# A convolution step rewritten on rows that ScalarE normalises, its mean put back at the end, in a four-pass transformer layer on one core

## The reference

```
x = x + attention(layernorm(x))                # with a second layer norm, gamma and beta inside
x = x + ffn(layernorm(x))                      # -> x2
x = x + s4d(layernorm(x))                      # -> x3: convolution along the axis of length 2
x = x + ffn(layernorm(x))                      # -> x4, the output

ffn(h)  = ((silu(h @ Wg * sg)) * (h @ Wu * su)) @ Wd * sd     # weights rounded to fp8 values
s4d(z)[0] = z[0] * (k0 + D)
s4d(z)[1] = z[1] * (k0 + D) + z[0] * k1        # only two taps, since the axis has two entries
```

## Time and profile before

| | us |
|---|---|
| median of three runs | 134.78 |
| the three runs | 134.71, 134.78, 136.53 |
| profiled execution, its own time | 134.78 |
| its span, first to last instruction | 133.0 |

### The profile page before, as it was taken

One profiled execution on the slowest core, in us unless ns is written; L12 is line 12 of the kernel. 1 busy time (PEld: TensorE's weight loads), 2 busy tenths in 40 slices (PEclk: granted clock), 3 DMA queues, 4 the chain that ended last, 5 costly groups with the idle time before them and its releaser, 6 DMA issues.

```text
span 133.0 us, 2063 instructions
## 1 busy us (share of the span) xinstructions
PE 117.5 (88%) x666; PEld 77.2 (58%) x666; DVE 104.6 (79%) x234; ACT 71.6 (54%) x132; POOL 88.6 (67%) x162
## 2 busy tenths in 40 slices
PE   5997979959999999999999997959999929999940
PEld 5884648528668768665577453446454517455630
DVE  0499999999973776857958999999999998456362
ACT  3225376817965468859653564954554633573500
POOL 2255899999998888963241756989999660049521
PEclk9999999999999999999999999999999999999999
DMA  4999800000000000000000000000000000002204
GB/s 99 312 327 384 267 4 2 0 0 5 0 2 0 2 0 5 0 0 0 0 0 5 0 0 0 0 2 5 0 0 0 0 2 0 5 0 79 79 0 158
DMA packets 5666, 5.80 MB, mean 44 GB/s; under 512 B 1124, under 2 KB 5144, under 8 KB 5656
## 3 DMA queue, kind: packets, MB, share of 16 engines
q1 hardware_dynamic: 4776, 5.65, 12.6%
q10 hardware_dynamic: 816, 0.02, 0.3%
q0 software_dynamic: 64, 0.02, 0.1%
HBM read 4.63 MB, written 1.05 MB: 43 GB/s over the span
## 4 chain that ended last, share of the span: by engine, by line
PE 43%; DVE 42%; issue 5%; ACT 3%; POOL 3%; DMA 2%; DVEq 0%; POOLq 0%; ACTq 0%
PE psum L1153 16%; PE psum L1168 8%; PE psum L1092 7%; DVE stats L652 6%; PE psum L1067 5%; DVE fused L917 4%; DVE scaled_down L865 3%; DVE down_raw L741 3%; DVE grid L732 3%; PE psum L1032 3%; DVE normed L888 3%; DMA x_in<-in_x 2%; DVE h_rows L906 2%; DVE grid L733 2%; PE psum L1114 2%
## 5 line engine op out<-in xcount | busy, mean ns | idle before, releaser
L436 POOL TENSOR_TENSOR f_tail<-fused,f_head 128x512 f16<-128x512 f32 x12 | 14.2, 1181 | 18.0 <-ACT f_head L614 18.0
L603 ACT ACTIVATE gated<-psum,scales 128x512 f32<-128x512 f32 x24 | 16.4, 683 | 15.8 <-PE psum L1153 15.8
L1168 PE MATMUL psum<-down,f_head 128*128 128x256 bf16 x96 | 22.0, 273 | 0.1
L1168 PE MATMUL psum<-down,f_tail 128*128 128x256 bf16 x96 | 22.0, 273 | 0.0
L917 DVE SCALAR_TENSOR_TENSOR fused<-psum,up_scales_fit,gated 128x512 f32<-128x512 f32 x24 | 17.6, 740 | 4.5 <-PE psum L1153 3.4
L614 ACT ACTIVATE f_head<-fused 128x512 f16<-128x512 f32 x24 | 15.0, 625 | 9.8 <-DVE fused L917 9.6
L1153 PE MATMUL psum<-h_head,up 128*128 128x512 f16 x48 | 14.3, 379 | 0.8 <-DVE fused L917 0.7
L924 DVE TENSOR_TENSOR f_tail<-fused,f_head 128x512 f16<-128x512 f32 x12 | 9.5, 790 | 6.2 <-ACT f_head L614 6.2
L1153 PE MATMUL psum<-h_tail,gate 128*128 128x512 f16 x48 | 14.3, 379 | 0.0
L1153 PE MATMUL psum<-h_tail,up 128*128 128x512 f16 x48 | 14.3, 379 | 0.0
L1153 PE MATMUL psum<-h_head,gate 128*128 128x512 f16 x48 | 14.3, 379 | 0.0
(11 more groups left out here) (169 smaller groups left out, 265.8 us busy)
## 6 DMA issues: line engine op xcount, KB each, us to landing
x_in<-in_x SPq DMA_DIRECT2D x4, 256.0 KB, 4.5
out<-x_in SPq DMA_DIRECT2D x4, 256.0 KB, 2.1
qkv_sb<-in_qkv SPq DMA_DIRECT2D x3, 256.0 KB, 4.3
gate_raw<-in_gate_w SPq DMA_DIRECT2D x1, 768.0 KB, 6.0
up_raw<-in_up_w SPq DMA_DIRECT2D x1, 768.0 KB, 7.8
down_raw<-in_down_w SPq DMA_DIRECT2D x1, 768.0 KB, 9.5
wo_sb<-in_o_proj SPq DMA_DIRECT2D x1, 256.0 KB, 5.3
down_scale_all<-in_down_scale SPq DMA_DIRECT2D x1, 128.0 KB, 9.3
```

What stands on the lines that cost most here:

```text
L436: pool.tensor_tensor(f_tail[:, m, :], fused[:, m % FUSED, :], f_head[:, m, :], ALU.subtract).then_inc(f_tail_by_pool, 1)
L603: act.activation(gated[:, m % 2, :], psum[:, BANK_GATE[m % 2], :], ACT.Silu, scale=gate_scales[:, m:m + 1]).then_inc(gated_ready, 1)
L1168: last = pe.matmul(column(BANK_DOWN[t // 2], H * (t % 2), H), part[:, m, t * P:t * P + P], down16[:, m, :], start=(m == 0 and t % 2 == 0 a ...
```

## The change

- x3 is kept without x2's mean. With z = (x2 - mean) * rstd and std = 1/rstd, x2 + tap0 * z = mean + (tap0 + std) * z. The layer norm behind it doesn't see the mean. So VectorE has one step per tile, (tap0 + std) * z, in place of two.
- z comes from ScalarE for all eight tiles (`z_rows`), in place of four (`x_lag`), and earlier in the pass. GpSimd computes std in `inverse_std` (one instruction more), and the negative mean term every time.
- The second tap's product now reads z of batch 0, and VectorE adds it in pass 2 (four additions more), in place of GpSimd's four `add_lag`.
- GpSimd adds all four residuals of pass 1 and 2; VectorE's `add_x1` goes. ScalarE normalises all four tiles for the next pass; VectorE's `norm_rows` go.
- The mean is put back in pass 3: ScalarE adds it for six tiles (`put_mean_back`), and VectorE's last two additions (`add_x3`) take it as a third operand. GpSimd's four residuals of pass 3 wait for ScalarE's first four.
- Voiding moves from VectorE's list in pass 2 to its list in pass 3, behind the first `fuse` and ahead of the four `scaled_down`; TensorE's sum for it moves from behind m = 1 of pass 2 to behind m = 0 of pass 3.
- In passes 1 and 2 GpSimd's tails are m = 1, 2, 4 in place of 1, 3, 4.

```
-                    residual(0, x2, x1, (first, first + 2, first + 3), x2_by_pool)
-                    inverse_std(2, first, 2, negative_mean=(n == 1))
+                    residual(0, x2, x1, range(first, first + T), x2_ready)
+                    inverse_std(2, first, 2, negative_mean=True, with_std=True)
+                    inverse_std(2, first + 2, 2, negative_mean=True, with_std=True)
+                    tail(n, POOL_TAILS[n][0])
+                    inverse_std(3, first, 2, negative_mean=True)
+                    tail(n, POOL_TAILS[n][1])
+                    inverse_std(3, first + 2, 2, negative_mean=True)
+                    tail(n, POOL_TAILS[n][2])
                     if n == 1:
...
+                        for t in range(T):
+                            lag_tap(t)
                 else:
-                    tail(n, POOL_TAILS[0])
+                    tail(n, POOL_TAILS[n][0])
                     if n == 3:
+                        pool.wait_ge(mean_back, T)
                         residual(1, x4, x3, range(T), x4_by_pool)
...
+            def z_rows(k):
+
+                act.wait_ge(shift_ready[2], k + 1)
+                act.activation(normed[:, k, :], x2[:, k, :], ACT.Identity, scale=rstd[:, 2, k:k + 1],
+                               bias=neg_mean_rstd[:, 2, k:k + 1]).then_inc(z2_ready, 1)
+
+            def put_mean_back(k):
+
+                act.activation(x3[:, k, :], x3[:, k, :], ACT.Identity, scale=1.0,
+                               bias=mean_var[:, 2, k, 0:1]).then_inc(mean_back, 1)
...
+                if n == 3:
+                    put_mean_back(T)
+                    put_mean_back(T + 2)
+                head(n, 5)
...
+            def convolve(tiles):
 
                 dve.wait_ge(taps_loaded, 1)
                 for k in tiles:
...
+                    dve.wait_ge(std_ready, k + 1)
+                    dve.wait_ge(z2_ready, k + 1)
+                    ins = dve.scalar_tensor_tensor(out=x3[:, k, :], in0=taps_all[:, 0, :], scalar=std[:, k:k + 1],
+                                                   in1=normed[:, k, :], op0=ALU.add, op1=ALU.mult)
...
                 for k in tiles:
...
+                    dve.wait_ge(lag_ready, k - T + 1)
+                    dve.tensor_tensor(x3[:, k, :], x3[:, k, :], x_lag[:, k - T, :], ALU.add).then_inc(x3_ready, 1)
...
             for n in range(2 * B):
                 if n >= 1:
                     h_tails(n)
+                if n == 3:
+
+                    fuse(n, 0)
+                    void_beyond()
+                if n >= 1:
...
-                    if n == 2 and m == 1:
+                    if n == 3 and m == 0:
                         pe.wait_ge(beyond_ready, 1)
...
-                if n == 2:
-                    pe.wait_ge(beyond_read, 1)
```

More of the change, by code:

```diff
@@ L119, in hybrid_layer @@
         one_rstd = sb("one_rstd", [P, K])
+        std = sb("std", [P, K])
         mean_rstd = sb("mean_rstd", [P, 4, K])
@@ L270, in load_s4d, with inverse_std @@
                                array.rearrange("(c p) n -> p c n", p=P)).then_inc(loaded, 16)
-            def inverse_std(n, k, count=1, twice=False, negative_mean=False):
+            def inverse_std(n, k, count=1, twice=False, negative_mean=False, with_std=False):
                 pool.wait_ge(stats_ready[n], k + count)
@@ L442, in residual, with lag_tap @@
                     pool.tensor_tensor(new[:, k, :], scaled_down[:, k, :], old[:, k, :], ALU.add).then_inc(ready, 1)
-            def lag_tap():
+            def lag_tap(t):
                 pool.wait_ge(taps_loaded, 1)
[L447 to L453, removed]
+                pool.wait_ge(z2_ready, t + 1)
+                pool.tensor_tensor(x_lag[:, t, :], normed[:, t, :], taps_all[:, 1, :], ALU.mult).then_inc(lag_ready, 1)
             for n in range(2 * B):
@@ L609, in _ @@
                 gate(n, 0)
[L610 to L631, removed]
@@ new lines, in _ @@
+                gate(n, 1)
+                head(n, 0)
+                if n == 0:
+                    copy_taps()
+                gate(n, 2)
+                head(n, 1)
+                if n == 0:
+                    for k in (T, T + 1):
+                        normalise(1, k, x1)
+                if n in (1, 2):
+                    z_rows(tiles[0])
+                    z_rows(tiles[1])
+                if n == 3:
+                    for k in range(T):
+                        put_mean_back(k)
@@ new lines, in _ @@
+                gate(n, 3)
+                if n in (1, 2):
+                    z_rows(tiles[2])
+                    z_rows(tiles[3])
+                head(n, 2)
+                if n == 0:
+                    for k in (T + 2, T + 3):
+                        normalise(1, k, x1)
+                gate(n, 4)
+                head(n, 3)
+                if n in (1, 2):
+                    normalise(3, tiles[0], x3)
+                    normalise(3, tiles[1], x3)
+                gate(n, 5)
+                head(n, 4)
```

134 lines of the change are left out of this document (58 added, 76 removed).

## The result

The changed kernel takes 130.81 us in the median (130.73 to 131.11, four runs); run beside it, the kernel before took 134.71 to 136.53. The ratio is 0.965, 95% interval 0.957 to 0.974: faster. Against that the gain is 3.9 us. The profiled executions say the same: 134.78 before, 130.82 now, spans 133.0 and 129.0. 133.6 was forecast, with a range from 130.2 to 135.6; what came is next to the first rival, 130.0.

The account below looks back on a forecast made before the run. VectorE was taken to bound passes 1 and 2, with GpSimd's list next. 1.9 us gained up to pass 3, less 0.7 and 0.05 lost there, made 134.78 - 1.15 = 133.6 us; 80% range 130.2 to 135.6.

Parts of the forecast that it names:

- the first rival: Passes 1 and 2: GpSimd meets VectorE hardly at all and TensorE bounds the passes; 130.0 us, chance 0.27.
- What bounded the kernel: Passes 1 and 2 before: VectorE never rests; TensorE loses 3.1 and 4.0 us, mostly ahead of the second transpose.
- VectorE stops being the bound, GpSimd's list is next: Passes 1 and 2: VectorE's busy time falls to 14.0 and 15.5 us, under TensorE's 16.5; GpSimd's list ends last.
- VectorE's links are ready 0.5 us ahead: VectorE's statistics and new steps would be ready about 0.5 us ahead of each inverse_std on GpSimd.
- GpSimd's free time: GpSimd's undisturbed list, from first residual to second transpose with ScalarE's two rows: 14.2 us.
- Waiting: GpSimd held up by VectorE: 0.3 for each of four inverse_std, 0.2 for tails, 1.4 us; pass 2 adds 0.4.
- The late last tail: End of passes 1 and 2: VectorE's last tail comes after TensorE wants it, losing 0.25 us each.
- Pass 3: 0.7 us lost, between 0 and 1.5, through ScalarE's added rows, a late last head and GpSimd's later residuals.
- The slower rival: Passes 1 and 2: GpSimd's short instructions are caught throughout, each inverse_std losing 0.86; about 140 us, chance 0.08.
- The third rival: Passes 1 and 2: GpSimd's pow blocks VectorE, which loses 1.4 us per pass; 135.4 us, chance 0.10.

Follow-up runs that it names:

- b_void_last: The kernel before with only the voiding moved, from pass 2 to behind the first fuse of pass 3: 133.53 us.
- a_pool_more: The changed kernel with one more unused 128x256 addition on GpSimd behind the first inverse_std for x3, in passes 1 and 2: 132.07 us.
- a_void_back: The changed kernel with voiding back in pass 2, ahead of the second pair's statistics: 132.99 us; two of its runs 132.10 and 132.32.
- a_dve_more: The changed kernel with two more unused statistics instructions on VectorE behind the first pair's statistics of x3, in passes 1 and 2: 132.00 us.
- a_two_steps: The changed kernel with the convolution in two VectorE steps again, without std, batch 1's z rows and putting the mean back: 136.67 us.
- a_early_stats: The changed kernel with the second tile's residual on VectorE again and the first pair's statistics of x2 ahead of the first fuse: 132.61 us.
- a_tail2_dve: The changed kernel with the tail of m = 2 on VectorE instead of GpSimd in passes 1 and 2: 131.65 us.
- a_tail2_pass1: The changed kernel with the tail of m = 2 on VectorE instead of GpSimd in pass 1 alone: 130.89 us.
- a_two_steps_wait: The kernel of a_two_steps with GpSimd's tails of m = 1 and 2 waiting for VectorE's first and second x3 pairs, passes 1 and 2: 134.12 us.

## Why the prediction was right, and where its sum was off

The time lies in the stated range, but not because the forecast was near: 1.15 us of gain were forecast, 3.9 came, and the forecast's own range began at 131.9. What holds 130.81 is the low end, 130.2, put there for the first rival at a chance of 0.27. So the order of events was foreseen and the size was not.

**What bounded the kernel**: right for pass 2, where b_void_last took VectorE's 1.6 us out and got 1.44 back; for pass 1 no run tests it alone. That most of TensorE's loss stands ahead of the second transpose holds for pass 2 (2.69 of 4.0 us) but not for pass 1 (1.33 of 3.1).

**VectorE stops being the bound, GpSimd's list is next**: right in pass 1, in the order and nearly in the instants. The chain runs through that list from 75.72 to 86.12 without a break, and a_pool_more shows it from the other side. In pass 2 the step "VectorE's links are ready 0.5 us ahead" failed: there VectorE's statistics and GpSimd's tail end together (102.27 and 102.22), and a_void_back and a_dve_more show that VectorE has nothing in hand.

**The size** was off in three terms, all to the safe side:
- GpSimd's free time: 14.2 forecast; 14.8 measured in pass 1, of which 0.95 is waiting for VectorE's instructions (0.37 in the `pow` at 78.24, the rest in the other two `inverse_std`, as the 0.52 for 0.19 at 84.13), so 13.85. In these 13.85 is a wait that the sum had no term for, 0.43 us for the statistics of x2 at 75.72. Residuals in a row take 0.70 each, where I read 0.76 from a row in which one of three had met VectorE's `add_x1`; std costs 0.15, not 0.28.
- Waiting: 1.4 forecast and 0.95 measured in pass 1. In pass 2, where 1.8 was forecast with the additions, it is 1.6: 1.2 in short instructions and twice 0.18 in tails. With the free time it makes 0.8 us in each pass.
- The late last tail, 0.25 in each pass: nothing. VectorE's tail at 87.79 took its free 0.69 us beside the taps' product, and TensorE didn't wait for it.

With this pass 2 starts 2.0 earlier (0.9 forecast) and pass 3 4.2 earlier (1.9 forecast), since GpSimd also enters pass 2 at 90.40 and not at 91.6.

**Pass 3**: forecast 0.7 lost, measured 15.59 us against 15.46 from its start to the first `scaled_down` at its end, so 0.13, which is TensorE's sum for the voiding. In ScalarE's timeline the four rows that put the mean back take 1.69 us, not 2.06, and the last head comes 13.48 us after the pass's start, against 13.15 before. The tail behind it is ready at 122.65 and TensorE wants it at 122.79. The 0.3 us were simply in hand.

```profile
114.08 1.69 ACT L615 ACTIVATE x_plus<-x_plus,mean_var 128x256 f32<-128x256 f32 x4
...
121.31 0.61 ACT L600 ACTIVATE f_head<-fused 128x512 f16<-128x512 f32 x1
```

**The rivals.** The first (hardly any meeting, 130.0) is the nearest in time, and its mechanism is half true: short instructions lost 0.95 and 1.2, not 0, and TensorE still waits 0.83 and 0.95 ahead of its transposes, but no step of VectorE was caught. It leaves out what decides this kernel. The slower rival priced the wrong victim: GpSimd's short instructions lost at most 0.39 each in the changed kernel's two passes, not 0.86, while VectorE's steps, caught by GpSimd's long tail, did lose 0.8 to 1.0 at a time, in five of the kernels tried (a_two_steps, a_dve_more, a_early_stats, a_tail2_dve, a_tail2_pass1). The changed kernel escapes that by 0.2 us in pass 1 and by 0.1 in pass 2, and this the prediction had no term for: it is luck. I worked with a mean wait where, for VectorE's steps, the truth is all or nothing. The third rival (`pow` blocks VectorE) is refuted once more: in the changed kernel VectorE's two steps at 78.66 took 0.87 beside a `pow` that stands from 78.24 to 79.31, and of which at most the first 0.37 us were waiting.

## What to carry to other kernels

When a list of short instructions on GpSimd and two-operand work on VectorE share a path, don't charge a mean for their contention: find the one long GpSimd instruction near a VectorE instruction on the path and ask which starts first, and by how much. If the margin is small, pin the order with a wait; here one or two waits per pass were worth 1.3 us in one kernel, 0.8 in another and 2.2 to 2.5 in a third, without any work taken away. And an unburdened engine's gain ends where the next list begins, so follow that list link by link, with durations of instructions in the same neighbourhood, not those that had met a neighbour.

## What the runs showed of the hardware

- A 128x2 `pow` on GpSimd takes 0.70 us free, 1.07 to 1.10 when a tail of VectorE (0.68) has started 0.15 to 0.2 us before it (78.06 and 78.24 in the changed kernel), and 1.24 when it has started 0.01 before (a_two_steps_wait, 77.95 and 77.96); yet VectorE's two-operand steps run at full pace beside it. It waits for VectorE at its start, and doesn't keep VectorE waiting afterwards. The Trainium skill, "SBUF — State Buffer", section "SBUF: two separate sides", has it that, where VectorE's instruction has two inputs in SBUF and GpSimd's reads SBUF, whichever starts first has the pair of ports that they share for its whole instruction. The 128x512 tails agree (1.16 us, and VectorE's step beside one takes up to 1.48 us in place of 0.48); the `pow` doesn't.
- Which of the two starts first can't be told from the records to 0.03 us: at 79.53 against 79.56 (a_two_steps) and 79.70 against 79.73 (a_early_stats) VectorE's step has the earlier start and is the one that is held. At 0.10 us (97.49 against 97.59, changed kernel) the earlier one wins.
- An ACTIVATE over 128x256 with the scale and bias of each row from SBUF came every 0.5 us (two in 1.08), one with a constant scale and a bias per row every 0.42 (four in 1.69).
- TensorE's clock can fall after waits of about a microsecond near the end of a pass: 1.23 and 0.97 us of them, then a granted clock of 0.52 for 3.3 us, in a_void_back's profiled run, and 0.67 and 0.76 over six us behind a wait of 2.16 in a_tail2_dve. Waits of 0.83 and 0.95 in the changed kernel left it at 1.00, and so did one of 2.69 in the profiled run of the kernel before. So a wait of TensorE can cost more than its own length. It needn't: two runs of a_void_back took 132.10 and 132.32 at a mean clock of 0.995 and 0.997. What lowered the clock in the later runs of the kernel before isn't shown, since none of them has a profile here.
